# Attention maxima found by one reduce over two PSUM banks, with the banks dealt out anew

## The reference, cut to what matters

```python
h = concat([tok(x, W), txt], axis=1)                  # (8, 1056, 64): 1024 image tokens and 32 text tokens
# attention, 4 heads of 16, for each of the 8 batch elements
q, k, v = split(layernorm(h) @ w_qkv.T)
attn = softmax(einsum('bhnd,bhmd->bhnm', q, k) * 16 ** -0.5, axis=-1)
h = h + proj(einsum('bhnm,bhmd->bhnd', attn, v)) + b_proj
# 8 experts, each token weighted by its two best gates
h = h + sum_e gate_e * (gelu(layernorm(h) @ W1[e] + b1[e]) @ W2[e] + b2[e])
```

## Time and profile before

| | |
|---|---|
| median of three runs | 852.92 us (852.79 to 853.16) |
| the profiled execution | 856.51 us, span 854.7 us |
| TensorE busy | 783.5 us, 92% |
| VectorE busy | 542.5 us, 63% |
| ScalarE busy | 460.8 us, 54% |
| 512 reduces of 512 columns (L1044) | 329.4 us busy, 683 ns each |
| 768 exponentials (L932) | 311.0 us busy, 466 ns each |

### The profile page before, as it was taken

The page is one execution under the profiler, slowest core; times in us unless marked ns, Lnnn a source line. Parts: engine busy times, 40 slices in busy tenths (PEclk is TensorE's granted clock), DMA queues, the critical chain, the costliest instruction groups (busy, mean ns, idle before and its releaser), DMA issues.

```text
span 854.7 us, 14341 instructions
## 1 busy us (share of the span) xinstructions
PE 783.5 (92%) x5352; PEld 304.7 (36%) x5352; DVE 542.5 (63%) x1181; ACT 460.8 (54%) x1069; POOL 131.6 (15%) x148
## 2 busy tenths in 40 slices
PE   1858899999999999999998999999988899999995
PEld 1342222433342243334224333433334344545442
DVE  5037664688876468887646588778864174656642
ACT  1100454566674456667445466766755655564662
POOL 0010100012000001201000110010100055463664
PEclk9955699999999999999999699999999999999998
DMA  9319121016621001662100110120000736465571
GB/s 194 76 52 196 58 59 38 2 48 143 112 79 66 1 2 58 133 112 86 59 2 1 41 53 2 48 97 1 15 2 2 140 81 133 101 133 100 118 140 26
DMA packets 61933, 60.03 MB, mean 70 GB/s; under 512 B 23840, under 2 KB 54056, under 8 KB 61864
## 3 DMA queue, kind: packets, MB, share of 16 engines
q1 hardware_dynamic: 59264, 57.58, 30.7%
q10 hardware_dynamic: 2599, 1.54, 0.9%
HBM read 38.88 MB, written 2.57 MB: 48 GB/s over the span
## 4 chain that ended last, share of the span: by engine, by line
PE 75%; DVE 14%; ACT 3%; DMA 3%; issue 2%; SPq 1%; POOL 0%; ACTq 0%; POOLq 0%; DVEq 0%
PE bank L1174 14%; PE bank L1196 13%; PE bank L1233 11%; PE bank L1210 8%; PE bank L1345 6%; PE bank L1328 6%; DVE max_parts L1044 5%; PE bank L1287 3%; PE bank L1179 2%; PE bank L462 2%; PE bank L513 2%; DMA q_stack<-m_part 1%; PE bank L638 1%; DMA proj_in<-in_L_attn_w_proj 1%; ACT probs L932 1%
## 5 line engine op out<-in xcount | busy, mean ns | idle before, releaser
L1044 DVE TENSOR_REDUCE max_parts<-bank 128x1 f32<-128x512 f32 x512 | 329.4, 683 | 123.4 <-PE bank L1233 121.9
L932 ACT ACTIVATE probs<-bank 128x384 f32<-128x384 f32 (+1 forms) x768 | 311.0, 466 | 175.8 <-PE bank L1196 174.1
L1196 PE MATMUL bank<-q_stack,k_stack 99*128 99x384 bf16 (+1 forms) x768 | 225.6, 322 | 2.7 <-ACT probs L932 2.4
L1233 PE MATMUL bank<-k_stack,q_stack 96*128 96x512 bf16 x512 | 205.2, 404 | 4.4 <-DVE max_tail L1052 1.8
L1174 PE MATMUL bank<-probs,v_tiles 128*32 128x384 f32 (+1 forms) x1536 | 156.4, 480 | 2.2 <-ACT heads_out L917 2.1
L1196 PEld LDWEIGHTS bank<-q_stack,k_stack 99*128 99x128 bf16 x768 | 72.0, 99 | 189.3 <-ACT probs L932 139.6
L984 ACT ACTIVATE hid<-bank,biases 128x704 f32<-128x704 f32 x96 | 77.7, 844 | 57.9 <-PE bank L1345 57.6
L1131 DVE SCALAR_TENSOR_TENSOR prod<-bank,biases,cwb 128x352 f32<-128x352 f32 x96 | 55.3, 580 | 64.6 <-PE bank L1328 54.8
L881 POOL TENSOR_TENSOR acc<-acc,prod 128x352 f32<-128x352 f32 x84 | 78.2, 931 | 59.7 <-DVE prod L1131 55.7
L861 POOL TENSOR_TENSOR part<-qk_rest,part 128x352 bf16<-128x352 f32 x24 | 20.4, 850 | 361.6 <-DVE part L1092 361.6
L1233 PEld LDWEIGHTS bank<-k_stack,q_stack 96*128 96x128 bf16 x512 | 50.6, 99 | 54.9 <-DVE max_parts L1044 30.3
(11 more groups left out here) (146 smaller groups left out, 541.9 us busy)
## 6 DMA issues: line engine op xcount, KB each, us to landing
cwb<-gates_by_expert SPq DMA_DIRECT2D x24, 704.0 KB, 11.3
x<-in_x SPq DMA_DIRECT2D x48, 256.0 KB, 6.9
q_stack<-part SPq DMA_DIRECT2D x48, 132.0 KB, 2.4
k_stack<-part SPq DMA_DIRECT2D x42, 132.0 KB, 2.5
x<-in_x SPq DMA_DIRECT2D x4, 576.0 KB, 11.3
h_res<-h_new SPq DMA_DIRECT2D x4, 528.0 KB, 3.0
recip<-recip_rows SPq DMA_DIRECT2D x32, 66.0 KB, 2.5
h_all<-h_res SPq DMA_DIRECT2D x4, 528.0 KB, 3.0
```

The lines of the kernel that those rows point to most:

```text
L932: nc.scalar.activation(probs[:, group % 3, h, 0:n], src, ACT.Exp, scale=SCALE).then_inc(exp_done, 1)
L1044: nc.vector.tensor_reduce(max_parts[:, c, H * j + h, i % 2:i % 2 + 1], src[:, :], AX.X, ALU.max)\
L1196: last = nc.tensor.matmul(bank[:, 0:n], ks[par][0:ROWS + 3, h, P * kt:P * kt + P], qs[par][0:ROWS + 3, h, QC[qc]], start=True, stop=True)
L1233: last = nc.tensor.matmul(bank[:, :], queries(h, j), ks[par][0:ROWS, h, HALF * (i % 2):HALF * (i % 2) + HALF], start=True, stop=True)
```

## The change

The two halves of the image keys are written by two matmuls into two neighbouring banks and reduced by one operation over 1024 columns. `max_bank` has two slots of two banks, taken in turn, in place of three of one bank; a maxima step waits for the reduce two steps back. The eight banks are dealt out as two for scores instead of three, one for P times V, four for maxima instead of three, one for side steps. A score unit so waits for the exponential two units back. `MAX_OF` falls to 13, 13 and 12 steps, `MAXU` to 41, and with it `MAX_PLACE` and the positions of the shifts move.

```diff
--- before.py
+++ after.py
@@ -40,7 +40,7 @@
 TPC = 3
 QR = H * TPC
 Q_TILES = [TPC, TPC, TPC - 1]
-MAX_OF = [2 * H * n + 1 for n in Q_TILES]
+MAX_OF = [H * n + 1 for n in Q_TILES]
 MAX_OF[-1] += NCH
 MAXU = sum(MAX_OF) + NCH
 PARTS = [(0, 0), (0, 1), (1, 0), (0, 2), (1, 1), (2, 0)]
@@ -184,9 +184,9 @@
 
         psum = ctx.enter_context(nc.psum_tensor("bank", [P, 8, 512], F32))
         banks = [psum[:, i, :] for i in range(8)]
-        score_bank = banks[0:3]
-        o_bank = banks[3]
-        max_bank = banks[4:7]
+        score_bank = banks[0:2]
+        o_bank = banks[2]
+        max_bank = [psum[:, 3 + 2 * i:5 + 2 * i, :].rearrange("p b l -> p (b l)") for i in range(2)]
         side_bank = banks[7]
 
         setup_loaded = sem("setup_loaded")
@@ -261,7 +261,7 @@
         ks = [sb_(f"k_stack{i}", [P, H, LP], BF16) for i, sb_ in enumerate((sbe, sb1))]
         v_tiles = [sb1(f"v_tiles{i}", [P, KT, H, 32]) for i in range(2)]
         v_tail = [sb1(f"v_tail{i}", [P, P]) for i in range(2)]
-        max_parts = sb1("max_parts", [P, NCH, QR, 3])
+        max_parts = sb1("max_parts", [P, NCH, QR, 2])
         max_tail = sb1("max_tail", [P, NCH])
 
 
@@ -437,14 +437,11 @@
 
         def max_slot(t, c, i, n):
 
-            if isinstance(t, int) and t == B - 1 and (c, i) == (NCH - 1, None):
-                return MAXU * B - 1, 0, MAXU * B - 1
+            if t == B - 1 and (c, i) == (NCH - 1, None):
+                t, n = B, 0
             t, n = (t + 1, n - MAXU) if n >= MAXU else (t, n)
-            at = MAXU * t + n - 1
-            if isinstance(t, int) and t == 0:
-                at = n if n < 2 else n - 1
-                return at, n % 3, at - 1 if n in (3, 4) else at - 2
-            return at, n % 3, at if n == 0 else at - 2
+            at = MAXU * t + n - (1 if t > 0 or n > 2 else 0)
+            return at, at % 2, at - 1
 
         ROOT_STEPS = 16
         chunk = [slice(c * CH, (c + 1) * CH) for c in range(NCH)]
@@ -920,7 +917,7 @@
                     qc, r = divmod(u, UPC)
                     n = QW[qc]
                     act.wait_ge(scores_ready, UNITS * b + u + 1)
-                    src = score_bank[u % 3][:, 0:n]
+                    src = score_bank[(UNITS * b + u) % 2][:, 0:n]
                     if r == 0:
                         nc.scalar.activation(probs_tail[qc][:, 0:n], src, ACT.Exp, scale=SCALE).then_inc(exp_done, 1)
                         return
@@ -1035,16 +1032,16 @@
                         c, i, n = i
                         at, place, _ = max_slot(t, c, i, n)
                         nt = Q_TILES[c]
-                        full_units = 2 * H * nt
+                        full_units = H * nt
                         dve.wait_ge(max_scores, at + 1)
                         src = max_bank[place]
                         parts = max_parts[:, c, :, :].rearrange("p (k h) n -> p k h n", h=H)
                         if i < full_units:
-                            h, j = divmod(i // 2, nt)
-                            nc.vector.tensor_reduce(max_parts[:, c, H * j + h, i % 2:i % 2 + 1], src[:, :], AX.X, ALU.max)\
+                            h, j = divmod(i, nt)
+                            nc.vector.tensor_reduce(max_parts[:, c, H * j + h, 0:1], src[:, :], AX.X, ALU.max)\
                               .then_inc(max_done, 1)
                         elif i == full_units:
-                            nc.vector.tensor_reduce(max_parts[:, c, 0:H * nt, 2],
+                            nc.vector.tensor_reduce(max_parts[:, c, 0:H * nt, 1],
                                                     src[:, 0:H * nt * TXT].rearrange("p (e l) -> p e l", l=TXT),
                                                     AX.X, ALU.max).then_inc(max_done, 1)
                         else:
@@ -1184,8 +1181,8 @@
                     n = QW[qc]
                     if r == 0:
                         pe.wait_ge(shifted, 16 * SHIFT_DMAS * (NCH * b + qc + 1))
-                    at_least(pe, exp_done, UNITS * b + u - 2)
-                    bank = score_bank[u % 3]
+                    at_least(pe, exp_done, UNITS * b + u - 1)
+                    bank = score_bank[(UNITS * b + u) % 2]
                     if r == 0:
 
                         for h in range(H):
@@ -1222,17 +1219,18 @@
                         at_least(pe, max_done, free)
                         bank = max_bank[place]
                         nt = Q_TILES[c]
-                        full_units = 2 * H * nt
+                        full_units = H * nt
 
                         def queries(h, j):
                             first = P * (TPC * c + j)
                             return qs[par][0:ROWS, h, first:first + P]
 
                         if i < full_units:
-                            h, j = divmod(i // 2, nt)
-                            last = nc.tensor.matmul(bank[:, :], queries(h, j),
-                                                    ks[par][0:ROWS, h, HALF * (i % 2):HALF * (i % 2) + HALF],
-                                                    start=True, stop=True)
+                            h, j = divmod(i, nt)
+                            for half in range(2):
+                                keys = slice(HALF * half, HALF * half + HALF)
+                                last = nc.tensor.matmul(bank[:, keys], queries(h, j), ks[par][0:ROWS, h, keys],
+                                                        start=True, stop=True)
                         elif i == full_units:
                             for e in range(H * nt):
                                 j, h = divmod(e, H)
```

## The result

The changed kernel takes 903.5 us (four runs, 897.4 to 905.1) against 853.0: a ratio of 1.055, with a 95% interval of 1.049 to 1.061. Forecast were 893, a range of 872 to 907, and slower. The way and the mechanism were right, the size was 10 us short, just past the 883 to 903 that the mechanism alone was given. The four runs of the changed kernel lie 7.7 us apart, and the shorter ones have the higher mean granted clock (897.4 us at 0.946, 905.1 at 0.932).

What follows compares the result with a forecast made beforehand. TensorE was taken as the bound, with three score banks only just enough. Terms 0.7 + 20.1 + 5.2 + 6.0 + 0.8 + 7.7 = 40.5 us gave 893 us against the median 852.9; range 872 to 907.

Steps and rivals of the forecast that it cites:

- The bound: Plain groups: TensorE waits for nobody, 2.18 of 2.20 us is work; three score banks are already only just enough.
- the turn of 0.92 us: Score ring, wide chunks: from a score's start until its bank is free again, so the third score can't start before 0.92.
- the fourth score's 1.30: Plain wide group: earliest start of the fourth score after the first; 1.54 with a pair behind the first, 1.52 behind the third.
- The formula by where the pairs stand: Plain wide groups with two score banks take 2.34 to 3.02 us by which scores have maxima pairs behind them; before 2.20.
- The reduce: VectorE: one reduce of 1024 costs 1.12 to 1.22 us, 1.13 taken; saves 23 us at most, worth nothing in the slots.
- The two slots: Maxima banks: asked for again after 2.8 us, ready in 1.8, so no wait; the old waits in the slots mostly go.
- prologue: Start of the kernel, where VectorE sets the time: +0.7 us together, first scores at 90.5 instead of 89.8.
- plain slots: Three slots with nothing else in them: +2.6, +1.2 and +2.9 by chunk, +6.7 a slot, +20.1 us in all.
- the faster rival: Score ring: two banks are enough, waits even out and 18 us of reduce waits go; 835 to 840 us, 8%.
- first chunks of 2, 4 and 6: Slots with values and finish steps, said to cover 0.6 of the 2.6 us ring loss: 2.0 each, 6.0 in all.
- the rival on the clock: New short idle spells in every group lengthen existing dips of the granted clock; two to four more give 904 to 915, 8%.
- The big reduce as bound: Maxima slots: TensorE also waits for them, some 0.2 us per pair in half of 256; +25 more, 905 to 918, 5%.

Runs made afterwards that it cites:

- score2: Kernel before with two score banks instead of three (third left empty), single maxima banks and reduces as before: 887.1 us, ratio 1.037.
- filled: Changed kernel plus 49 score matmuls nobody reads, behind the last slot's score units once its maxima are done: 896.5 us, ratio 1.045.
- before_filled: Kernel before, three score banks, with the same added unread score matmuls in the last slot: 859.6 us, ratio 1.006.
- two_reduces: Changed kernel with each pair of banks reduced by two operations over 512 columns instead of one over 1024: 904.7 us, ratio 1.057.
- timed: Kernel before with maxima steps placed by VectorE's time per step over TensorE's time per unit, instead of evenly by score columns: 854.6 us, ratio 1.001.
- merged3: Kernel before, three score and three maxima banks, a pair's matmuls in their own units but reduced by one operation: 926.0 us, ratio 1.077.
- merged4: Changed kernel with the two maxima matmuls of a pair in units of their own, two score and four maxima banks: 896.8 us, ratio 1.047.
- moved: Changed kernel with maxima steps moved from behind a group's fourth score to behind the third: 890.9 us, ratio 1.044.

## Why the prediction was right, and where it was short

*The bound.* That TensorE stood full in the plain groups and that three score banks are only just enough: shown. With two, alone, the time rises by 34 us (score2), and the turn of 0.92 us and the fourth score's 1.30 are read in the trace to 0.01. Of the 150 or so groups that wait, a few were read one by one; the rest is by chunks.

*The places.* The formula by where the pairs stand gives 3.02, 2.78, 2.58 and 2.56; measured 3.00, 2.79, 2.57 and 2.57. Moving pairs by one unit gave 12.6 us back, where the same formula had said 10 to 17. That is the second part of the loss, beside the ring itself.

*The reduce.* A pair costs 1.17 back to back (twelve in 14.13, the last 1.22 long), between the bounds, not at the 1.13 that I chose:

```profile
69.31 14.13 DVE L1041 TENSOR_REDUCE max_parts<-bank 128x1 f32<-128x1024 f32 x12 [11.92 <-PE bank L1232]
...
87.11 0.27 DVE L1080 CAST m_part<-bank 36x128 bf16<-36x128 f32 x1
```

The shift's copy comes at 87.1 instead of 85.9, and the first scores at 91.0: +1.2 for the +0.7 of the sum. From one execution to the next that start moves as much: it is 89.5 in filled, whose prologue is the same, and 88.7 in before_filled, so this term can't be told from the spread. VectorE's 10 us less, with 15 to 25 forecast, agree with the pair's 1.17: it saves 0.04 to 0.05 against two single reduces and not 0.09. That it is hidden in the slots is shown by two_reduces.

*The two slots.* Hardly a wait for them outside the prologue (0.7 us): right. The reason given for the old waits going, that short units are now spaced like long ones, isn't needed: they go in score2 too, from 16.9 to 1.9 us, with the old spacing. The sums of the plain slots came out near: +2.2, +1.1 and +2.6 against +2.6, +1.2 and +2.9. That the old waits are 18 us to be had was the faster rival's price. timed took some 6 us off them (16.9 to 10.5 at the big maxima matmuls) and was no faster; more than that no run here shows.

*The sum, term by term* (spans, before to after): prologue 1.2 (0.7 said); plain slots 17.6 (20.1); first chunks of slots 0 and 7 5.2 (5.2); first chunks of 2, 4 and 6 9.1 (6.0); middle chunks 0.5 (0.8); other last chunks 10.3 (7.7); experts 1.5 (0). Together 45.4 where I had 40.5. Three terms were mis-sized. The plain slots were put 2.5 too high. The steps for values and finish cover nothing of the ring: 3.0 a chunk, where I took 0.6 off the plain chunk's 2.6. And the last slot's last chunk, put at +1.8, took +7.8, because the granted clock fell to 0.67 in it; with the clock at 1.00 it is +2.4 (20.6 us in two_reduces). That was the rival on the clock, in a place that I hadn't named: it fell not in the long stretches that I had in mind but where no maxima are left to fill the waits. Filling them gave 7 us back (filled). Against it, one of the chunks with roots came out 1.6 shorter instead of 1.0 longer, because before had its long dip there. Without the 5.4 us of the clock the sum is 40.0 for 40.5; that it comes so near is partly luck, as +3.1 for the values chunks and +1.5 for the experts cancel against plain slots and last chunks that were put too high. Between the medians the loss is 50.5 and not 45.5: the profiled execution of before lay 3.5 us above its median (it has the long dip of the clock in the earlier trace rows), that of the changed kernel 1.5 below. Its four runs spread over 7.7 us, and in each the time goes with the mean clock (897.4 us at 0.946, 902.0 at 0.939, 905.0 and 905.1 at 0.934 and 0.932); in which chunk the clock fell is known for the profiled one alone.

*The rivals.* That two banks are enough is refuted (score2), and the waits stand where the block of P times V was said to put them. The big reduce as bound: not in the changed kernel (two_reduces), but where the two matmuls of a pair stand apart and share a bank with the next pair (merged3), in part also with banks of their own (merged4).

## What to carry to other kernels

Count a ring of buffers by its turn (from one use of a buffer until it is free for the next) against the work that the producer has between two of its uses, not by averages: here one block of 0.78 us made a turn of 0.92 too long for two banks although two units took 1.10 on average. When a buffer is taken from one ring for another, price both rings; the instruction that was improved was hidden and the ring that paid for it was on the path. What must wait anyway should stand beside other work: moving a step by one unit was worth 12.6 us without a single instruction less.

## What the runs showed of the hardware that was not expected

A reduce of 1024 columns from two neighbouring PSUM banks takes 1221 ns, one of 512 683 to 684: 538 ns for 512 columns more, 1.05 ns each; an estimate of the fixed part from these two is 145 ns, and it is paid once. Back to back it is 1.17 against 2 times 0.61, so a pairing saves VectorE 0.04 to 0.05 us a pair and not 0.09.

Short waits went with a low clock. In the last chunk of the last slot TensorE's longest idle at a score is 0.4 us, and yet the changed kernel was granted 0.67 on average there (half speed for some 17 of 26 us), and moved 0.54; with the waits filled by idle work it was 1.00. It isn't a rule: the same waits of TensorE ran at 1.00 in the profiled execution of two_reduces, busy for 17.2 of 20.6 us, and so did the plain slots of the changed kernel, busy for 20.2 of 21.6 us in the first chunk and 18.7 of 20.2 in the last. In merged3, where TensorE waited 0.68 and 0.84 us for the shared bank in the rows above, it fell in three of the plain first chunks and not in a fourth. The four runs of the changed kernel, 897.4 to 905.1 us, show what such falls are worth with nothing changed in the kernel.
